# Fourth attention: units of one token tile from each of two batches, values folded as full blocks, outputs as pairs of 64-row matmuls, four norm tiles inside the first units

## The reference, cut to what matters

```python
x = x + tanh(g_xattn[3]) * xattn3(layernorm(x), ctx, mask, ...)
x = x + tanh(g_ffn[3]) * ffn3(layernorm(x), ...)

def xattn3(h, c, mask, q_w, k_w, v_w, o_w, q_norm_w, k_norm_w):   # 32 heads of 128, 8 key/value heads
    q = rmsnorm(heads(h @ q_w.T), q_norm_w)      # (4, 32, 256, 128)
    k = rmsnorm(heads(c @ k_w.T), k_norm_w)      # (4, 8, 64, 128), each used by 4 heads
    v = heads(c @ v_w.T)
    attn = softmax(q @ k^T / sqrt(128) + mask)
    return merge(attn @ v) @ o_w.T
```

## Time and profile before

| | |
|---|---|
| median of 3 runs | 1484.44 us (1483.86 to 1485.25) |
| span of the profiled execution | 1484.5 us |
| PE busy in the span | 1327.8 us (89%) |
| DVE busy | 1157.6 us (78%) |
| ACT busy | 720.5 us (49%) |
| POOL busy | 337.5 us (23%) |

### The profile page before, as it was taken

How to read it: one execution, slowest core, us unless ns; L and a number is a source line. 1 busy time by engine, 2 the same in 40 slices (tenths; PEclk the granted TensorE clock), 3 DMA queues, 4 the chain that set the end, 5 groups by cost and what they waited for, 6 DMA issues and landing times.

```text
span 1484.5 us, 18579 instructions
## 1 busy us (share of the span) xinstructions
PE 1327.8 (89%) x6364; PEld 982.2 (66%) x6364; DVE 1157.6 (78%) x2109; ACT 720.5 (49%) x1517; POOL 337.5 (23%) x386
## 2 busy tenths in 40 slices
PE   7999999999998989978999998999999999998104
PEld 5665566566586558746888876777777777777102
DVE  4788988898888997976555567677677677777998
ACT  4777777787523443433222235555464555553104
POOL 1112112121255020143111022221321212212620
PEclk9999999999999999988999998999999999998557
DMA  5678987798820011243211310210101101000001
GB/s 221 168 176 179 246 216 173 191 243 201 214 76 1 1 57 35 51 94 80 72 43 42 105 64 1 72 42 30 71 3 70 72 0 72 1 1 1 1 0 57
DMA packets 37910, 127.73 MB, mean 86 GB/s; under 512 B 4944, under 2 KB 10960, under 8 KB 31680
## 3 DMA queue, kind: packets, MB, share of 16 engines
q1 hardware_dynamic: 26304, 83.38, 16.1%
q0 software_dynamic: 11520, 43.26, 15.4%
HBM read 72.63 MB, written 10.75 MB: 56 GB/s over the span
## 4 chain that ended last, share of the span: by engine, by line
PE 51%; DVE 25%; ACT 7%; DVEq 6%; issue 4%; DMA 4%; POOL 1%; POOLq 0%; SPq 0%
PE PS L150 10%; PE PS L152 10%; PE PS L151 10%; DVE AR L676 4%; PE PS L939 4%; PE PS L976 3%; DMA AR<-AR 3%; ACT s_sb L606 2%; DVE AR L2679 2%; DVE AR L2668 2%; DVE AR L2675 2%; DVEq L666 2%; PE PS L962 1%; DVE AR L682 1%; PE PS L535 1%
## 5 line engine op out<-in xcount | busy, mean ns | idle before, releaser
L438 POOL DMA_DIRECT2D AR<-AR x76 | 74.5, 1094 | 327.4 <-DMA AR<-AR 132.9
L1242 DVE TENSOR_TENSOR R16r<-PS,R16r 64x512 fp32r<-64x512 f32 x128 | 88.1, 689 | 56.7 <-ACT R16r L1097 55.8
L151 PE MATMUL PS<-R16r 128*128 128x512 f32 (+1 forms) x328 | 122.0, 372 | 0.0
L535 PE MATMUL PS<-R,PT 128*128 128x512 f32 x256 | 116.1, 596 | 3.6 <-DVE X L716 3.6
L152 PE MATMUL PS<-R16r 128*128 128x512 f32 (+1 forms) x312 | 119.1, 382 | 0.0
L510 PE MATMUL PS<-R,HT 128*128 128x256 f32 x512 | 116.5, 381 | 2.3 <-ACT R L595 2.0
L510 PEld LDWEIGHTS PS<-R,HT 128*128 128x128 f32 x512 | 94.8, 190 | 15.3 <-ACT R L595 3.7
L606 ACT ACTIVATE s_sb<-PS,sm 128x64 f32<-128x64 f32 x256 | 77.9, 336 | 52.7 <-DVE sm L701 52.2
L1097 ACT CAST R16r<-PS 64x512 fp32r<-64x512 f32 x128 | 74.3, 580 | 49.8 <-PE PS L939 49.0
L1102 ACT COPY AR<-PS 128x512 f32<-128x512 f32 x64 | 37.5, 585 | 124.2 <-PE PS L152 124.2
L150 PE MATMUL PS<-HTr,R16r 128*128 128x512 f32 (+1 forms) x240 | 90.9, 379 | 4.2 <-DVE R16r L190 2.7
(11 more groups left out here) (321 smaller groups left out, 3562.4 us busy)
## 6 DMA issues: line engine op xcount, KB each, us to landing
AR<-AR POOLq DMA_DIRECT2D x76, 528.0 KB, 6.8
OR<-in_wo SPq DMA_DIRECT2D x12, 1024.0 KB, 12.1
dequantised<-AR SPq DMA_DIRECT2D x8, 1056.0 KB, 5.5
WR<-in_w0q SPq DMA_DIRECT2D x8, 1024.0 KB, 11.5
AR<-in_w3q SPq DMA_DIRECT2D x8, 1024.0 KB, 7.0
WR<-dequantised SPq DMA_DIRECT2D x22, 256.0 KB, 2.7
AR<-in_nf SPq DMA_DIRECT2D x4, 1056.0 KB, 9.4
nf_in<-in_nf SPq DMA_DIRECT2D x4, 1056.0 KB, 10.7
```

Source lines behind the costliest of these rows:

```text
L151: nc.tensor.matmul(out, ah, bl, start=False, stop=False)
L438: nc.gpsimd.dma_start(nf_below(g)[:, part], what[:, part], accum_op=ALU.add, max_dma_last_dim=4 * N_NF // 2).then_inc(added, 16)
L535: i = nc.tensor.matmul(bank(5 + tt), PT[:, at:at + P], vo[:, pr, b, :], start=pr == 0, stop=pr == 1)
L1242: i = nc.vector.tensor_tensor(VOl[rows, h // 2, b, :], bank(7)[rows], VOh[rows, h // 2, b, :].bitcast(F32), ALU.subtract)
```

## The change

- **Units.** A group G (now 16) is one key/value head for two batches: G // 8 says which two, G % 8 which head. Unit u = (G, tt) does tile tt of both batches: its first tile (o = 0) is of the even batch, its second (o = 1) of the odd one. The first 16 units serve tiles 0 to 3, the last 16 tiles 4 to 7. Weights are loaded and split once per G, so once in 2 units, 16 times instead of 8; keys and values are computed for 128 context rows at a time.
- **Folds.** VO is stored as the whole 128x512 block of one head for the two batches (rows 0 to 63 one batch, 64 to 127 the other). One ACT copy and one DVE subtraction per fold; no swapped copy, no swapped squares. There are still 64 folds; none in slots 0 and 1 of even units, one in slot 2, three in odd units.
- **Outputs.** A tile is contracted with its own batch's 64 rows only, one head at a time: 4 heads x 3 products x 2 tiles = 24 matmuls of 64 rows x 512 columns per unit, in pairs that use rows 0 to 63 (bank 5) and rows 64 to 127 (bank 6). They come as heads (0, 1), then `turn_q` and `turn_k`, then heads (2, 3).
- **Start.** Norm tiles 4 to 7 (of token tiles 4, 6, 5, 7) move from the start into units 0 to 3: transposes into bank 7, and PE waits for their low part before it goes on. `keys_values(1)` moves to before unit 0, and so do the splits of the second group's query weights; the first fold moves ahead of the first queries.
- **Order on DVE.** Low parts of the slot-2 folds go ahead of both adds, and both adds come after the whole outputs. The statistics of tiles 0 to 3 move from the last units to units 18 and 20; those of tiles 4 to 7 are all taken in unit 31 or after it.

The diff, cut to its core:

```diff
+        TILE_ORDERS = {6: (0, 2, 1, 3, 4, 6, 5, 7), 7: (0, 1, 2, 3, 4, 6, 5, 7)}
...
+            if n == 6 and t >= 4:
+                return bank(7)
...
-        PIECES3 = 10
+        PIECES3 = 6
...
-        VOh = R16r[:, 4096:8192].rearrange("p (r b n) -> p r b n", r=2, b=B)
-        VOl = R16r[:, 8192:12288].rearrange("p (r b n) -> p r b n", r=2, b=B)
+        VOh = R16r[:, 4096:8192].rearrange("p (q h n) -> p q h n", q=2, h=HG)
+        VOl = R16r[:, 8192:12288].rearrange("p (q h n) -> p q h n", q=2, h=HG)
...
+        def tile3(u, o):
+
+            return T // 2 * (u // NUH) + 2 * o + u % 2
...
         def folds(u, slot):
...
+            G, tt = divmod(u, 2)
+            if G + 1 == NHG:
                 return []
+            if tt == 0:
+                return [(G + 1, 0)] if slot == 2 else []
+            return [(G + 1, slot + 1)]
...
-            pool_norm(pool, 6)
+            pool_norm_pair(pool, 6, 0)
+            pool_norm_pair(pool, 6, 1)
             query_scale(0)
+            split_q(1, (0, 1))
             query_scale(1)
+            split_q(1, (2, 3))
+            pool_norm_pair(pool, 6, 2)
+            pool_norm_pair(pool, 6, 3)
...
-            def outputs(u, tt):
-                g, b = divmod(u, B)
-                if tt == 0:
+            def outputs(u, heads):
+
+                G = u // 2
+                if heads[0] == 0:
                     pe.wait_ge(A3["pt_lo"], u + 1)
-                    pe.wait_ge(A3["piece_lo"], 8 * g + 4 * (b // 2) + 4)
...
-                for pr in range(2):
-                    at = (pr * 2 + tt) * P
-                    i = mm3(bank(5 + tt), PTh[:, at:at + P], PTl[:, at:at + P], VOh[:, pr, b, :], VOl[:, pr, b, :],
-                            pr == 0, pr == 1)
-                i.then_inc(A3["out_mm"], 1)
+                for h in heads:
+                    cols = slice(h * P, (h + 1) * P)
+                    for k, (p, v) in enumerate(((PTh, VOh), (PTh, VOl), (PTl, VOh))):
+                        for o in range(2):
+                            rows = slice(SK * o, SK * (o + 1))
+                            i = nc.tensor.matmul(bank(5 + o), p[rows, cols], v[rows, G % 2, h, :],
+                                                 start=h == 0 and k == 0, stop=h == HG - 1 and k == 2)
+                            if h == HG - 1 and k == 2:
+                                i.then_inc(A3["out_mm"], 1)
+
+            def late_norm(r, k):
+                previous_piece(r)
+                pe_norm_tile(pe, 6, k)
...
+                if u < 4:
+                    late_norm(PIECES3 * (G + 1) + (3 * tt + K_AT), u + 4)
+                    pe.wait_ge(lo_ready, lows(6) + u + 5)
                 for f in folds(u, 1):
                     fold_outputs(*f)
-                outputs(u, 0)
+                outputs(u, (0, 1))
                 if more:
                     turn_q(u + 2, 1)
-                if b == 2 and g + 1 < NG:
-                    turn_k(g + 1)
-                outputs(u, 1)
+                if tt == 0 and G + 1 < NHG:
+                    turn_k(G + 1)
+                outputs(u, (2, 3))
                 for f in folds(u, 2):
                     fold_outputs(*f)
                 if more:
                     scores(u + 2)
-                if b == 1 and g + 1 < NG:
-                    keys_values(g + 1)
+                if tt and G + 2 < NHG:
+                    keys_values(G + 2)
...
-            def folded_high(g, bp, h):
-                act.wait_ge(A3["piece_mm"], PIECES3 * g + vo_at(bp, h) + 1)
-                for rows, b in fold_halves(bp, h):
-                    i = nc.scalar.copy(VOh[rows, h // 2, b, :], bank(7)[rows])
-                i.then_inc(A3["piece_hi"], 1)
+            def folded_high(G, h):
+                act.wait_ge(A3["piece_mm"], PIECES3 * G + 2 + h + 1)
+                nc.scalar.copy(VOh[:, G % 2, h, :], bank(7)).then_inc(A3["piece_hi"], 1)
...
             for u in range(NU0):
-                g, b = divmod(u, B)
+                G, tt = divmod(u, 2)
...
                 if u + 1 < NU0:
                     shift(u + 1)
                 probs_low(u)
+                if u == 0:
+                    scaled((4, 5))
...
+                if u < 4:
+                    low((u + 4,))
+                if u < 2:
+                    scaled((u + 6,))
                 for f in folds(u, 1):
                     folded_low(*f)
-                add(u, 0)
-                if u == NU0 - 1:
-                    dve.drain()
-                    nc.vector.bn_stats(st[:, T - 2, :], X[:, T - 2, :])
                 if more:
                     square_sum(u + 2, 1)
-                add(u, 1)
                 for f in folds(u, 2):
                     folded_low(*f)
-                if g == NG - 1 and b < B - 1:
-                    dve_stats(dve, b)
+                add(u, 0)
+                add(u, 1)
+                if u in (NUH + 2, NUH + 4):
+                    dve_stats(dve, (u - NUH) // 2 - 1)
```

More of the change, by code:

```diff
@@ L908, in piece, with keys_values @@
                 return bank(7)
-            def keys_values(g):
-                o = piece(PIECES3 * g) if g else bank(6)
-                pe.wait_ge(A3["kv_in"], 16 * (g + 1))
-                for j in range(2):
-                    for c in range(C):
-                        at = c * 2 * DH
-                        nc.tensor.matmul(o[:, j * P:(j + 1) * P], CT[:, c, j * P:(j + 1) * P], WKV3[:, at:at + DH],
-                                         start=c == 0, stop=c == C - 1)
+            def keys_values(G):
+                o = piece(PIECES3 * G) if G else bank(6)
+                pe.wait_ge(A3["kv_in"], 16 * (G + 1))
+                two = slice(G // NG * SKP, (G // NG + 1) * SKP)
+                for c in range(C):
+                    at = c * 2 * DH
+                    nc.tensor.matmul(o[:, 0:DH], CT[:, c, two], WKV3[:, at:at + DH], start=c == 0, stop=c == C - 1)
@@ L918, in keys_values @@
                 for c in range(C):
                     at = c * 2 * DH + DH
-                    i = nc.tensor.matmul(o[:, 256:512], WKV3[:, at:at + DH], CT[:, c, :], start=c == 0, stop=c == C - 1)
+                    i = nc.tensor.matmul(o[:, DH:DH + SKP], WKV3[:, at:at + DH], CT[:, c, two],
+                                         start=c == 0, stop=c == C - 1)
                 i.then_inc(A3["piece_mm"], 1)
-            def turn_k(g):
-                o = piece(PIECES3 * g + K_AT) if g else bank(2)
-                pe.wait_ge(A3["kn_ready"], g + 1)
-                for j in range(2):
-                    i = nc.tensor.transpose(o[:, j * P:(j + 1) * P], kvs[:, j * P:(j + 1) * P], ident[:])
-                i.then_inc(A3["piece_mm"], 1)
@@ L930, in fold_outputs, with turn_k @@
-            def fold_outputs(g, bp, h):
-                r = PIECES3 * g + vo_at(bp, h)
+            def turn_k(G):
+                o = piece(PIECES3 * G + K_AT) if G else bank(2)
+                pe.wait_ge(A3["kn_ready"], G + 1)
+                nc.tensor.transpose(o[:, 0:P], K_ROWS, ident[:]).then_inc(A3["piece_mm"], 1)
+            def fold_outputs(G, h):
+                r = PIECES3 * G + 2 + h
                 o = piece(r)
@@ L942, in queries @@
[L942 to L949 removed]
+                if h == 0:
+                    pe.wait_ge(A3["o_in_odd" if G % 2 else "o_in"], 16 * (G // 2 + 1))
+                    pe.wait_ge(A3["piece_hi"], PIECES3 * G + 1)
@@ new lines, in fold_outputs, with queries @@
+                nc.tensor.matmul(o, V_TURNED, wo3(G)[:, h * D:(h + 1) * D], start=True, stop=True)\
+                    .then_inc(A3["piece_mm"], 1)
+            def queries(u, o):
+                G, tt = divmod(u, 2)
+                if u:
+                    pe.wait_ge(A3["q_sq"], 2 * u - 1 + o)
+                t = tile3(u, o)
+                if G == 0:
+                    pe.wait_ge(lo_ready, lows(6) + TILE_ORDERS[6].index(t) + 1)
+                elif G == NG:
+                    pe.wait_ge(lo_ready, lows(7))
+                tok = slice(t * P, (t + 1) * P)
+                hi, lo = wq3(G)
@@ L1080, in keys_values @@
-            def keys_values(g):
-                act.wait_ge(A3["piece_mm"], PIECES3 * g + 1)
-                src = bank(7 if g else 6)
-                nc.scalar.copy(kvs[:], src)
-                blocks = src[:, 256:256 + B * SK].rearrange("p (r o k) -> p r o k", r=B // 2, o=2)
-                turned = SWAPPED.rearrange("p (r o k) -> p r o k", r=B // 2, o=2)
-                nc.scalar.copy(turned[:, :, 0], blocks[:, :, 1])
-                nc.scalar.copy(turned[:, :, 1], blocks[:, :, 0]).then_inc(A3["piece_hi"], 1)
@@ L1115, in query_turned, with keys_values @@
-            def query_turned(u, tt):
-                act.wait_ge(A3["tq_mm"], 2 * u + tt + 1)
-                nc.scalar.copy(QT3[:, tt * 512:(tt + 1) * 512], bank(2)).then_inc(A3["qT_ready"], 1)
+                    nc.scalar.copy(wq3(G)[0][:, c], WQ3[:, c * WQ:(c + 1) * WQ]).then_inc(A3["q_hi"], 1)
+            def keys_values(G):
```

(6 more changed lines are left out.)

409 lines of the change are left out of this document (198 added, 211 removed).

## The result

The changed kernel takes 1515.26 us (median of 4 runs, 1514.53 to 1515.60), the kernel before 1484.41 beside it: 1.0200 times as long, 95% interval 1.0187 to 1.0213. That is 30.9 us slower. The forecast was 1507.0 with a range of 1474 to 1534: slower was right and the time lies in the range, but 8 us of the loss were not in the forecast. A run's time lies some 2 us above its span (1515.48 us for 1513.7 here; 1487.78 for 1485.7 in a later run of the kernel before), so the profiled execution of before, with its span of 1484.5, was probably a little slower than the median run.

The account below looks back on a forecast made before the run. The prediction took PE to bound the stage, so relief of ACT and DVE wins only PE gaps. Terms -6.7 + 2.4 + 0.5 + 13.4 + 11.4 + 2 + 2.5 - 2 = +23.5 on 1484.5 gave 1507 us, range 1474 to 1534.

Parts of the forecast that it names:

- The kv wait: Before `keys_values` in the loop: PE's 0.96 us wait for the last fold's low part goes, in 15 places, -6.7 us.
- Keys and values: In the loop: 14 `keys_values` calls of about 1.89 us replace 7 of 3.43, +2.4 us.
- `turn_k` +0.5: Turning of the keys: comes twice as often with half the transposes, its own wait small, +0.5 us.
- Outputs as pairs: Output matmuls: pairs of 64 rows at 0.23 us, plus array shape changes, 64 times 0.21 = +13.4 us; bounds 0 to 26.
- in and out together: At both ends of each output block: changing array shape and back costs 0.14 to 0.24 us, read from other partial-array matmuls.
- the other estimate in the prediction: Output blocks: four exposed drains per unit, from a documented 166 ns constant beyond streaming, make 21 us; not used.
- Norm tiles: Units 0 to 3: PE waits for norm tiles' low parts, 9.6 us, with the transposes +11.4 us; bounds 1.8 to 18.
- clock +2: Units 0 to 3: a low clock after the norm-tile wait, priced at 4 us, at even odds +2 us.
- The start: Before unit 0: PE gaps before folds 1 to 3 and `keys_values(1)` start unit 0 later, +2.5 us; bounds -6 and +6.
- the gap of 4.13 and the slow clock: In the start: the largest PE gap, before a fold, and the low clock after it were both to go.
- The end: Last units: two pairs of statistics leave DVE's way (-2.9), both adds come after the last outputs (+0.75): -2 us.
- the faster one: Start and norm tiles: waits close, clock stays up, shape changes cost under about 0.1 us: 1478.5 us; chance 0.20.

Follow-up runs that it names:

- the run that reached unit 0 at full clock: Changed kernel with keys_values(1) behind scores(1), fold copies and fold 2's low part earlier, exponential ahead of the key copy: 1508.71 us, ratio 1.0152 to the kernel before.
- the repeat: The changed kernel run once more with no edit: 1518.26 us, ratio 1.0207 to the kernel before.
- the last run of the new units: Changed kernel with reordered start, norm tiles in old banks, one output block per unit, ACT/DVE reordered, even units' weight copies before fold copies: 1493.45 us, 1.0051 times before.

## Why the prediction was right or wrong

The bound was read rightly: the stage is PE's, and 43.5 us off DVE and 25.9 off ACT gained only the waits before `keys_values`. By the terms of the sum, against the +29.2 us of the spans:

- **The kv wait, -6.7:** right. Neither `keys_values` nor anything next in line waits in the steady units.
- **Keys and values, +2.4, `turn_k` +0.5:** too dear. A call takes 1.76 us in the loop and not 1.89, so 14 calls against 7 of 3.43 make +0.6; the single transpose of the keys takes 0.20 us and its wait does not show.
- **Outputs as pairs, 64 x 0.21 = +13.4:** the mechanism was right, its size was not, and this is the largest miss of the sum. The pairs themselves run at 0.23 us as forecast, with both members at once. A block costs 0.35 us by the run that adds one. The steady period gives 0.31: +0.82 for two units, +0.48 for the kv wait that is gone, less 0.05 for keys and values, is 1.25 over 4 blocks. For 64 blocks that is 20 to 22 us. The failing step was "in and out together cost 0.14 to 0.24", taken from half arrays of 64 columns and from quarter arrays; for halves of 64 rows it is 0.35. That lies in the stated bounds of 0 to 0.4, and the other estimate in the prediction, 21 us from four exposed drains per unit, came nearer than the one that was used.
- **Norm tiles, +11.4 and clock +2:** measured +9.6 (69.13 less four steady units of 14.895). The waits are 2.52, 1.51, 1.60 and 1.50 us, where the sum had 4.3, 1.5, 2.3 and 1.5; the odd units were right. In unit 0 PE came later than forecast, for its first queries took 4.00 us behind the low clock (921.40 to 925.40) and not 2.98; the run that reached unit 0 at full clock waited 2.94. The other 1.4 us of the 4.3 no run explains. The clock, put at even odds, did not fall there: 1.00 from 924 to 962 us. It did in the run where this wait was 2.94 (0.57 over 924 to 928).
- **The start, +2.5:** +7.1 to `turn_p(0)`, and +7.4 to the first queries of unit 0, the point that the +2.5 was counted to (921.40 against 911.96, less the 2.0 that came from ahead of the stage). Both lie outside the term's own bounds of -6 and +6. The four gaps were forecast at 2.9, 2.3, 2.1 and 2.5 (9.8 in all) and are 2.54, 1.89, 1.96 and 2.33 (8.7), which is 1.1 less. Two things were missing. One is the clock: the sum said "the gap of 4.13 and the slow clock go", and the slow clock came twice. By rows at both levels, 6 query records, the fold and four transposes take 4.4 us from 895.92 where they take 2.8 at full clock; from 916.73, the value part takes 1.39 (0.82) and the scores 3.28 (1.73): 3.7 us up to the first queries, and 1.2 more in these. The other is the waits ahead of the first fold, 6.07 us for 2.85, which the sum did not have: +3.2. Two small waits of before (0.56 and 0.39) went, uncounted. Together that is 4.8 of the 4.9 us missed. No run tested why the waits ahead of the first fold grew.
- **The end, -2:** measured -0.9 with the last units in it. These are four more units at +0.41, so the end itself gave about -2.5; in the repeat, whose rest is 163.1 us, about -1.1.

The terms as measured, -6.7, +0.6, 20, 9.6, 7.1 and -2.5, make 28 of the 27.2 us that remain without the shift of +2.0 ahead of the stage. The forecast lies 8.3 us under the result. Of these, 1.0 is the sum of 1508.0 taken down to 1507, though it was the start, said there to round up, that came out dearer; 1.6 is what the medians differ by beyond the spans; 5.7 is between the sum of +23.5 and the +29.2. In it outputs make +7 and the start +5, keys and norm tiles -6, the end -0.5, and the shift +2. So that the result came within 8 us is in part luck: 11 us of costs that were missed met 6 that were overstated.

The rivals: the faster one needed the start's waits closed and shape changes under 0.1 us, and neither held. The runs with the start reordered and the norm tiles moved show how much of its first half was to be had by order: the start comes to 1.7 us under the kernel before at best (54.38 to 52.66; the rival had -6), the norm tiles to +1.7 (the rival had 6). No version with the new units came under the kernel before: with both repairs and the single block it is at 1.0051. Of the 0.23 us per unit that are left there, 0.1 is the hidden wait of the odd units; the rest, and the 1.7 us of transposes in the first units, is PE's work. No run removed that last wait, but by these numbers the units as such lose here.

One thing stays open: the clock can explain the place of the first `keys_values` only in part, for the repeat has 0.96 over 440 to 480 us and yet comes to it at 864.34.

## What to carry to other kernels

Where PE has hardly a gap, count what a new layout adds to PE first, the changes of array shape among it, and take relief of ACT and DVE at the size of the PE gaps that it closes. Price a change of shape by adding one more of them in a run, for its cost from blocks of other shapes came out 0.6 of the true one. And before a layout is rebuilt for a wait, try the wait's own cure: moving one step in a hand-written order took away most of the largest wait, and another about half of the next, for a kernel 0.8% faster; each such move also decides what POOL and DVE do late a few steps on. And where the clock can fall, look at more than one profile: one kernel's start differed by 1.5 us between executions by the clock alone.

## What the runs showed of the hardware

- The granted clock fell after gaps of 2.54 and 2.33 us on PE (0.57 and 0.51 in the stretches behind), not only after one of 4.13; it stayed at 1.00 behind 2.52 us in unit 0, and in the reordered start of before with gaps of 1.58 and 1.45. In the repeat it also fell behind three waits of 1.02, 1.13 and 0.94 close together, and in the first profile of the same kernel, behind the same waits, it did not. The length of one gap alone does not tell it.
- Two 64-row matmuls on split operands start together and both last 0.50 or 0.39 us; a pair costs the 0.23 us of one full matmul. Issued as two sets of six, the second set starts 0.57 us after the first, and the block takes 2.17 us instead of 1.59.
- A change between the full array and halves of 64 rows is paid on both sides, 0.18 us going in and 0.15 coming out, by single records beside four transposes; a whole block more costs 0.35. The transposes between two blocks bear most of it: 0.59 for four, against 0.36 in the kernel before.
- The modelled end of matmuls can hide a wait from the idle column: in the last run of the new units 0.19 us in each odd unit, seen only in the distance of starts (0.62 for 0.43).
- A subtraction of 64 rows x 512 takes as long as one of 128 rows: 0.689 us both, by the 128 of the earlier trace rows and the 64 of after. For the ACT copies it is 0.580 and 0.588.
